# Attention probabilities of the even heads transposed by DMA in a one-core transformer block with routed experts

## The reference, cut to what matters

```
q = LN(x) @ Wq; k, v = split(ctx @ Wkv)          # 16 heads of 64, a null key/value in front
attn = softmax(q * 64**-0.5 @ [nk, k].T)         # 256 x 257 per head
x += tanh(g) * LN(attn @ [nv, v] @ Wout)
x += tanh(g) * ffn_fp8(LN(x))                    # 256 -> 1024 -> 256, relu, fp8 hidden
x += tanh(g) * (rms(LN(x)) @ W_in.T + decayed patch scan of ctx)
x += tanh(g) * top2_experts(LN(x))               # 8 experts, gelu gate
```

## Time and profile before

| | |
|---|---|
| median of 3 runs | 1578.78 us (1574.91 to 1578.94) |
| the profiled execution | 1575.19 us, span 1573.4 us |
| PE busy | 1455.4 us, 92% of the span |
| DVE busy | 1200.8 us, 76% |
| ACT busy | 927.6 us, 59% |
| POOL busy | 635.8 us, 40% |
| mean granted TensorE clock | 0.981 |
| DMA | 93.44 MB, mean 59 GB/s |

### The profile page before, as it was taken

One profiled execution on the slowest core, in us unless ns is written; L12 is line 12 of the kernel. 1 busy time (PEld: TensorE's weight loads), 2 busy tenths in 40 slices (PEclk: granted clock), 3 DMA queues, 4 the chain that ended last, 5 costly groups with the idle time before them and its releaser, 6 DMA issues.

```text
span 1573.4 us, 36260 instructions
## 1 busy us (share of the span) xinstructions
PE 1455.4 (92%) x12542; PEld 1073.2 (68%) x12542; DVE 1200.8 (76%) x3275; ACT 927.6 (59%) x2530; POOL 635.8 (40%) x773
## 2 busy tenths in 40 slices
PE   2999999999999999999999999999967899999997
PEld 2667676767677776767677776767645666666665
DVE  6578888898989898888989898888875545454443
ACT  4476676767676767667676767767654432333332
POOL 6201333424342434424242424334234566555553
PEclk7999999999999999999999999999987999999999
DMA  8202020120202020211202020201232634333231
GB/s 265 86 1 69 10 74 22 61 75 9 81 2 82 2 81 15 69 49 34 82 2 81 2 82 8 75 23 41 73 109 91 188 65 64 57 61 53 50 61 22
DMA packets 78176, 93.44 MB, mean 59 GB/s; under 512 B 21312, under 2 KB 61776, under 8 KB 78000
## 3 DMA queue, kind: packets, MB, share of 16 engines
q1 hardware_dynamic: 51488, 73.21, 14.0%
q0 software_dynamic: 15680, 17.78, 6.9%
q10 hardware_dynamic: 10832, 0.13, 0.4%
HBM read 60.70 MB, written 31.30 MB: 58 GB/s over the span
## 4 chain that ended last, share of the span: by engine, by line
PE 52%; DVE 32%; ACT 9%; issue 4%; DMA 1%; POOL 1%; ACTq 0%; SPq 0%; POOLq 0%; DVEq 0%
PE S L1190 11%; PE W L1137 8%; PE W L1139 8%; PE W L1138 7%; DVE mx L1796 6%; PE O L1212 5%; PE T L1142 5%; ACT prob L956 4%; DVE pTl L1808 3%; PE O L1303 3%; PE S L1275 2%; PE W L1142 2%; DVE st_ln L1767 1%; DVE nm L1799 1%; ACT prob L965 1%
## 5 line engine op out<-in xcount | busy, mean ns | idle before, releaser
L956 ACT ACTIVATE prob<-S,nm 128x256 f32<-128x256 f32 x512 | 235.9, 475 | 88.0 <-DVE nm L1799 87.7
L753 POOL TENSOR_SCALAR ve_ln<-mv_ln 128x2 f32<-128x2 f32 x64 | 14.4, 225 | 534.5 <-DVE mv_ln L1770 534.5
L949 ACT ACTIVATE pTh<-T 128x512 f16<-128x512 f32 x256 | 139.4, 596 | 115.9 <-PE T L1142 107.9
L1808 DVE SCALAR_TENSOR_TENSOR pTl<-T,pTh 128x512 f16<-128x512 f32 x256 | 164.1, 680 | 9.9 <-ACT pTh L949 9.9
L1796 DVE TENSOR_REDUCE mx<-S 128x2 f32<-128x512 f32 x256 | 163.1, 678 | 9.1 <-PE S L1275 9.0
L1190 PE MATMUL S<-GL,xgh 128*128 x568 | 168.9, 379 | 0.1
L716 POOL DMA_INDIRECT out_dram<-ysb,tab x71 | 112.6, 1586 | 114.7 <-issue 67.0
L965 ACT ACTIVATE prob<-prob,rden 128x256 f32<-128x256 f32 x256 | 116.2, 501 | 71.3 <-DVE p0n L1817 71.3
L1142 PE MATMUL T<-ident,prob 128*128 128x128 f32 x1024 | 141.9, 283 | 0.4 <-DVE prob L1823 0.3
L1137 PE MATMUL W<-cTh,Wkh 128*128 128x256 f16 x512 | 140.5, 274 | 0.0
L1138 PE MATMUL W<-cTl,Wkh 128*128 128x256 f16 x512 | 140.5, 274 | 0.0
(11 more groups left out here) (311 smaller groups left out, 4364.3 us busy)
## 6 DMA issues: line engine op xcount, KB each, us to landing
cx<-in_ctx_dram SPq DMA_DIRECT2D x16, 512.0 KB, 5.3
gst<-in_L_ffn_gating_w_dram SPq DMA_DIRECT2D x16, 512.0 KB, 6.2
gating_split<-gsp SPq DMA_DIRECT2D x16, 512.0 KB, 2.7
GL<-gating_split SPq DMA_DIRECT2D x8, 1024.0 KB, 5.2
stg<-in_L_xattn_Wkv_dram SPq DMA_DIRECT2D x8, 512.0 KB, 13.5
xl<-in_x_dram SPq DMA_DIRECT2D x16, 256.0 KB, 4.2
lst<-in_L_ffn_linear_w_dram SPq DMA_DIRECT2D x16, 256.0 KB, 5.2
xres<-in_x_dram SPq DMA_DIRECT2D x16, 256.0 KB, 2.7
```

Source lines behind the costliest of these rows:

```text
L949: A(flat(pTh[:, h, :, :]), T[h][:, :], ACT.Copy).then_inc(s_pTh[h], 1)
L956: ins = A(prob[:, h, t, :], S[h][:, t * NTOK:(t + 1) * NTOK], ACT.Exp, bias=nm[:, h, t:t + 1], scale=SM, accum_out=rs[:, h, t:t + 1])
L1808: V.scalar_tensor_tensor(flat(pTl[:, h, :, :]), T[h][:, :], 1.0, flat(pTh[:, h, :, :]), ALU.mult, ALU.subtract).then_inc(s_pTl[h], 1)
```

## The change

The even head's probabilities no longer go through PE. ACT's `norm` writes them normalized as fp16 high rows (ph) from prob and rden, ahead of the odd head's normalization; DVE's new `even_prob_low` writes the low rows (pl). The sync queue transposes both by two DMAs of 128x512 fp16, SBUF to SBUF, into eTh and eTl, which are double over the pairs. `values` waits for the two DMAs and for the odd head's pTl. The odd head stays as it was: four transposes, one pTh, one pTl. DVE no longer normalizes the even head.

In the order of the engines: `even_prob_low(j)` is placed in each slot, in slots 1 and 5 behind add_residual and decayed, in slots 2 and 4 ahead of attn_low, in slot 7 behind the fourth norm. In slot 2 x1T's high and low parts move ahead of the norm; in slot 3 the norm stands between the two halves of the relus (before: ahead of all four); in slot 7 x4T's copy moves ahead of v's last high part. SP's transfers are spread over the pairs, since each pair now has its two waits there.

Five buffers share homes: sq with hq, x2 with x1, xhTh/xhTl with x1Th/x1Tl, dech with onehot, decl with cum.

```diff
-        pTh, pTl = sb("pTh", [P, 2, 2, NTOK], FP16), sb("pTl", [P, 2, 2, NTOK], FP16)
+        pTh, pTl = sb("pTh", [P, 2, NTOK], FP16), sb("pTl", [P, 2, NTOK], FP16)
+        eTh, eTl = [], []
+        for i in range(2):
+            eTh.append(sb(f"eTh{i}", [P, TT, 2, P], FP16))
+            eTl.append(sb(f"eTl{i}", [P, TT, 2, P], FP16))
+        ph, pl = sb("ph", [P, TT, NTOK], FP16), sb("pl", [P, TT, NTOK], FP16)
...
+            def even_probs_T(g):
+
+                at_least(sp, s_pv, g - 1)
+                sp.wait_ge(s_ph, g + 1)
+                sp.dma_start_transpose(eTh[g % 2][:, :, :, :].rearrange("p t k r -> p (t k) r"),
+                                       ph[:, :, :].rearrange("p t k -> p (t k)")).then_inc(s_eTh[g % 2], 16)
+                sp.wait_ge(s_pl, g + 1)
+                sp.dma_start_transpose(eTl[g % 2][:, :, :, :].rearrange("p t k r -> p (t k) r"),
+                                       pl[:, :, :].rearrange("p t k -> p (t k)")).then_inc(s_eTl[g % 2], 16)
...
+                for j in range(PAIRS):
+                    g = i.n * PAIRS + j
+                    if j == 0 and i.n > 0:
+                        gating_out(i.n - 1, gates_of[i.n - 1])
+                    if j == 1:
+                        if i.n > 0:
+                            linear_out(i.n - 1)
+                        if i.n > 1:
+                            x4_out(post.shift(-1))
+                    if j == 2:
+                        if i.n == 0:
+                            sp.wait_ge(s_setup, 1)
+                        sp.dma_start(lst[:, :, :], pick(lin_v, i.n)).then_inc(s_lw, 16)
+                        if loads:
+                            sp.wait_ge(s_nrm["ln1"], i.n + 1)
+                            sp.dma_start(xl[nxt.par][:, :, :], pick(x_v, nxt.n)).then_inc(s_x[nxt.par], 16)
+                    if j == 3 and loads:
+                        sp.wait_ge(s_u, i.n + 1)
+                        sp.dma_start(cx[nxt.par][:, :, :], pick(ctx_v, nxt.n)).then_inc(s_c[nxt.par], 16)
+                    if j == 4:
+                        sp.dma_start(gst[:, :, :], pick(gat_v, i.n)).then_inc(s_gw, 16)
+                    if j == 5:
+                        if post_:
+                            sp.wait_ge(s_xb, i.n)
+                        sp.dma_start(xres[:, :, :], pick(x_v, i.n)).then_inc(s_xr, 16)
+                    if not pre and j in (3, 5, 6):
...
+                        expert_in((3, 5, 6).index(j))
+                    if j == PAIRS - 1 and post_:
+                        x3_out(post)
+                    even_probs_T(g)
...
                 def norm(j):
-                    act.wait_ge(s_rden, i.n * 8 + j + 1)
+                    g = i.n * PAIRS + j
+                    act.wait_ge(s_rden, g + 1)
+                    at_least(act, s_eTh[(g - 1) % 2], 16 * ((g - 1) // 2 + 1))
+                    for t in range(TT):
+                        ins = A(ph[:, t, :], prob[:, 0, t, :], ACT.Copy, scale=rden[:, 0, t:t + 1])
+                    ins.then_inc(s_ph, 1)
                     for t in range(TT):
                         ins = A(prob[:, 1, t, :], prob[:, 1, t, :], ACT.Copy, scale=rden[:, 1, t:t + 1])
-                    ins.then_inc(s_prob[1], 1)
+                    ins.then_inc(s_prob, 1)
...
+                    g = i.n * PAIRS + j
+                    pe.wait_ge(s_eTh[g % 2], 16 * (g // 2 + 1))
+                    pe.wait_ge(s_eTl[g % 2], 16 * (g // 2 + 1))
+                    pe.wait_ge(s_pTl, g + 1)
...
+                                if h:
+                                    rhs = (pTl if n == 1 else pTh)[:, kt, :].rearrange("p (t r) -> p t r", r=P)
+                                else:
+                                    rhs = (eTl if n == 1 else eTh)[g % 2][:, :, kt, :]
...
+                def even_prob_low(j):
+                    g = i.n * PAIRS + j
+                    at_least(dve, s_eTl[(g - 1) % 2], 16 * ((g - 1) // 2 + 1))
+                    dve.wait_ge(s_ph, g + 1)
+                    for t in range(TT):
+                        ins = V.scalar_tensor_tensor(pl[:, t, :], prob[:, 0, t, :], rden[:, 0, t:t + 1],
+                                                     ph[:, t, :], ALU.mult, ALU.subtract)
+                    ins.then_inc(s_pl, 1)
...
-                    for t in range(TT):
-                        ins = V.tensor_scalar(prob[:, 0, t, :], prob[:, 0, t, :], rden[:, 0, t:t + 1], None, ALU.mult)
-                    ins.then_inc(s_prob[0], 1)
```

More of the change, by code:

```diff
@@ L570, in step @@
                 post, nxt = i.shift(-1), i.shift(2)
+                pre, attn, post_ = PRE in parts, ATTN in parts, POST in parts
+                loads = pre and i.n + 2 < NB
+                if attn:
+                    gates_of[i.n] = work.at["gT"]
                 if i.n == 1:
                     sp.wait_ge(s_blank, 16 * TT * (NB - FIRST_BATCHES))
-                if ATTN in parts and PRE in parts:
-                    wait_apart(sp, s_nrm["ln1"], i.n + 1)
-                    wait_apart(sp, s_u, i.n + 1)
@@ L576, in step @@
[L576 to L611, removed]
+                if not attn:
+                    if i.n == NB:
+                        gating_out(NB - 1, gates_of[NB - 1])
+                        linear_out(NB - 1)
+                        x4_out(post.shift(-1))
+                        sp.wait_ge(s_pv, PAIRS * NB)
+                        sp.wait_ge(s_go, 16 * NB)
+                        sp.wait_ge(s_lo, 16 * NB)
+                        for e in range(early, E):
+                            expert_in(e)
+                        x3_out(post)
+                        x4_out(post)
+                    if loads:
+                        sp.dma_start(xl[nxt.par][:, :, :], pick(x_v, nxt.n)).then_inc(s_x[nxt.par], 16)
+                        sp.dma_start(cx[nxt.par][:, :, :], pick(ctx_v, nxt.n)).then_inc(s_c[nxt.par], 16)
+                    return
@@ L945, in prob_high @@
                 def prob_high(j):
[L946 to L949, removed]
+                    act.wait_ge(s_pT, i.n * 8 + j + 1)
+                    at_least(act, s_pv, i.n * 8 + j)
+                    A(flat(pTh[:, :, :]), T[1][:, :], ACT.Copy).then_inc(s_pTh, 1)
                 def exps(j):
@@ L981, in v_high, with relus @@
                     one("v", m, vh[nxt.par][:, m // 2, (m % 2) * 512:(m % 2 + 1) * 512], 1 / WS)
-                def relus():
-                    for m in range(4):
+                def relus(units=(0, 1, 2, 3)):
+                    for m in units:
                         k, nfull, _ = work.at["w1"][m]
@@ L1069, in step @@
                             k_high(1)
+                        if post_:
+                            one("x1T", 0, flat(x1Th[:, :, :]))
                         if attn:
@@ L1075, in step @@
                             attn_high(0)
-                        if post_:
-                            one("x1T", 0, flat(x1Th[:, :, :]))
                         if pre:
@@ L1080, in step @@
                             q_high(3)
-                    if j == 3 and post_:
-                        relus()
+                    if j == 3:
+                        if post_:
+                            relus((0, 1))
+                        if attn:
+                            norm(j)
+                        if post_:
+                            relus((2, 3))
                     if j == 4:
@@ L2064, in step @@
                             pick_boundaries()
-                    if j == 3 and post_:
-                        boundaries()
+                    if j == 3:
+                        if attn:
+                            even_prob_low(j)
+                        if post_:
+                            boundaries()
                     if j == 4:
```

95 lines of the change are left out of this document (57 added, 38 removed).

## The result

The changed kernel took 1625.65 us, the median of 4 executions (1619.95 to 1631.56), and the kernel before, on the same chip, 1576.85 (1574.05 to 1578.94). The ratio is 1.031, with a 95% interval of 1.027 to 1.035: 49 us slower, where 9.5 us faster was forecast. 1626 lies above the range as well.

What follows compares the result with a forecast made beforehand. PE looked like the bound (68.9 of 71.5 us a step) with DVE close behind. 14 steps at 0.6 us gave 8.4, about 1 more came from step 0, 0 from step 15: 1578.8 - 9.5 = 1569 us, range 1540 to 1612.

Steps and rivals of the forecast that it cites:

- the price of even_prob_low: DVE's two low-row operations a pair were taken at 0.80 us, bounds 0.52 and 1.43 (slowed while POOL writes).
- the walk: Follows one full step from msel through each pair's maxima to the next msel; 9.5 us faster overall, chance 0.42.
- the sum of -0.6 us a step: At the next msel, a full step was to end 0.6 us earlier; 14 such steps give 8.4 us.
- The first and the sixth: Starts of the maxima of pairs 1 and 6, forecast at +0.27 and -0.1 us against before.
- 775.3 against 773.2: End of pair 7's values if transposes take 5 us to land, against before; given as +2.2 us a step.
- the terms of maxima(7): Before pair 7's maxima: division done 758.3, ph, odd norm, vh, aTh 2.8, aTl 0.6; given as +0.3 us.
- The landing L: From end of even_prob_low until values may start: 3.2 us, bounds 1.9 and 6; with 3.2 nothing waits.
- The queueing term: Part of the landing time: 0.3 us for the low rows' transfer queueing on SP, issue taken as some 0.33 us.
- The list of covers: Landing time each slot stands without delay: 3.3 to 5.0 us, slot 7 (3.45) said to go first.
- rival (2): Transposes land late: gain gone from 4.0 us, at 5 us +2.2 a step and 1610 us; chance 0.27.
- Rival (1): PE is the bound after all, ACT and DVE having more slack: -3.7 us a step, 1519 us; chance 0.12.
- No change: Landing between 3.6 and 4.2 us, or ACT's extra work cancelling DVE's saving: 1575 to 1583 us; chance 0.17.

Runs made afterwards that it cites:

- pool_quiet: Changed kernel with GpSimd's xb, x2b, uh, ul, lst, lsp, dech and decl operations cut to 16 columns from step 2 on; 1587.3 us, ratio 1.009.
- before_quiet: Kernel before the change with the same GpSimd operations as in pool_quiet cut to 16 columns from step 2 on; 1565.1 us, ratio 0.994.
- no_transfers: Changed kernel without its 256 transposing DMAs, even values reading the odd head's transposed rows; ph and pl still written; 1606.7 us, ratio 1.020.
- short_both: no_transfers with both ph and pl over 16 of 256 columns; 1559.5 us, ratio 0.991.
- short_low: no_transfers with even_prob_low (pl) over 16 of its 256 columns; 1576.8 us, ratio 1.000.
- short_high: no_transfers with ACT's ph over 16 of 256 columns from step 1 on, pl whole; 1578.0 us, ratio 1.0015.
- rest_alone: Changed kernel without ph and pl, both heads transposed on TensorE as before; shared homes, spread loads and new order kept; 1580.3 us, ratio 1.004.

## Why the prediction was wrong

**The sum was made per engine with durations of undisturbed rows.** The step that failed is the price of even_prob_low and of DVE's operations around it in the walk, and with it the sum of -0.6 us a step. Its 0.80 us is right in six of the eight slots of the step (0.85 to 0.88 by duration, as in the row at 739.08) and wrong in slot 4 (1.24) and slot 5 (1.69, above even the bound of 1.43). The wait for ph ahead of it was seen by the walk in part only: 1.74 us of idle DVE in slot 3 and 1.05 in slot 6 of this step. The walk took every other duration as it stood in before, but xn went from 0.73 to 1.24, dec from 0.85 to 1.07 and xh from 1.43 to 1.56. xn shows how: POOL's xb add starts 7.91 us behind msel in both kernels, but xn started 9.07 behind it and now starts at 8.55, since the even normalization ahead of it is gone. The 0.52 us that the change saved there moved xn into POOL's add, and 0.51 were paid back at once. In the kernel before the two rows are (DVE's timeline, then POOL's)

```profile
710.52 0.73 DVE L1777 TENSOR_SCALAR xn<-xl,mv_ln,rstd_ln 128x256 f32<-128x256 f32 x2
```

```profile
709.36 1.41 POOL L775 TENSOR_TENSOR xb<-xres,bi_b 128x256 f32<-128x256 f32 x2
```

The cause is shown by pool_quiet against before_quiet: 29 of the 49 us.

The trace fits a lock that is held for a whole instruction: over the run a slowed operation ends a fixed time behind the end of a POOL instruction, den 0.02 us, p0n 0.03, xn and xh 0.15, pl 0.28 (30 of 39 slowed ones), dec 0.55. pTl runs beside POOL too and keeps its 0.68. The exception is the second pl of slot 4, nine times over the run: in the walked step it takes 0.83 us and ends 0.60 ahead of POOL's dec (773.34). For it the rule isn't shown. The Trainium skill, "SBUF — State Buffer", SBUF: two separate sides, states such a rule: a DVE operation with two SBUF inputs and a GpSimd operation that reads SBUF take the same port pair in turn, and the loser waits. pl, dec, p0n and den agree with it; xn and xh have one tensor input and are slowed as well. The rule speaks against this change, which replaces a pTl that reads PSUM by a pl that reads SBUF twice, and the prediction should have weighed it.

**Point by point**, the starts of the maxima against before, aligned at msel (before at 701.45 + 27.91 = 729.36), forecast and measured. The third row is pool_quiet against before_quiet, in the same step, where pool_quiet has the full clock and no wait for a landing:

| | maxima(1) | (2) | (3) | (4) | (5) | (6) | (7) | next msel |
|---|---|---|---|---|---|---|---|---|
| forecast, us | +0.27 | 0 | +0.4 | -0.4 | +0.2 | -0.1 | +0.3 | -0.6 |
| measured, us | +0.78 | +0.83 | +1.1 | +0.18 | +0.44 | +1.6 | +2.0 | +1.4 |
| GpSimd quiet, us | +0.27 | +0.07 | +0.33 | -0.60 | +0.20 | -0.14 | -0.36 | -1.02 |

The first and the sixth are the mis-sized ones: +0.5 by xn, and +1.5 in slot 5 by dec, pl and xh. The walk's shape was right, and with GpSimd quiet its numbers are too, to 0.2 us up to maxima(6): what it had wrong is what DVE's operations take beside GpSimd. bnd no longer waits for PE, as forecast; the +0.7 and more of slots 1 to 3 is partly taken back at maxima(4), and PE's saving is lost where the walk lost it, at xh: PE idle 1.43 us there in this step, "near 1" forecast, now joined by 1.14 ahead of logits. Two slips in the prediction's sums change nothing: 775.3 against 773.2 is 2.1, not 2.2, and the terms of maxima(7) give +0.2, not +0.3.

**The landing L.** Forecast 3.2 us; 2.4 to 2.5 in the median, plus the wake-up, for which the forecast took 0.2 us from no row (in the changed kernel PE starts 0.09 us behind the landing that it waited for), so the central value was on the safe side. The queueing term was mis-sized in another place: SP needs 1.20 us to issue one transpose, not the 0.33 of the earlier trace rows, and beside GpSimd's scatters they land in up to 9.5 us, beyond the bound of 6. PE waited for them 28 us in 11 places by the list of waits, and 7.5 us in four more that the profile puts down to "issue", though each ends 0.09 us behind a landing of eTl. Nothing of this was forecast in slots 0 to 6, and it was in slot 3 that it came in 11 of the steps 2 to 14, not in slot 7. The list of covers said so: slots 1 and 3 had the least, 3.3 us, and slot 7 had 3.45. Of 1309 ns a block (the Trainium skill, "VectorE: DVE Perf Modes", The three transpose paths) this trace shows less than half: four blocks land 2.4 us after the issue, near the 2.1 us of a plain transfer of twice the bytes out of SBUF, as the Trainium skill, "Advanced Engine Details and Errata", X-Bar Transpose (TRN2), has it.

**What rival (2) got right.** It ended on the slower side by a mechanism that exists: with waits in PE, ACT and DVE it is worth up to 19 us. It is the smaller part. Its 1610 was reached without it: no_transfers is at 1606.7.

**The clock** was no term of the walk. Behind idle gaps of 1.43 us ahead of xhT and 1.14 ahead of logits came at least 2.4 us at the 1.2 GHz level. It was left at nothing without a reason, though the walk itself forecast a longer idle gap of PE: in no_transfers a step with such a stretch takes 1.3 us more than one without.

**Rival (1)** fell: PE as the bound would give 1519, and even short_both gives 1559.5. **No change** would have been met only by work that is left out (short_low, short_high).

The steps between the runs are 6 us the rest of the change, 26 ph and pl net of TensorE's saving, 9 the transfers with ACT's and DVE's waits for them, 10 PE's waiting for them. That they add up to the difference says nothing, since each run starts where the last one ends. The 29 us of meeting GpSimd, and what the clock costs, cut across these parts and aren't added to them. What stays open: the order on ACT that costs rest_alone its 6 us was read from the trace, and no run undid it alone.

No version of the changed kernel came out faster than the one before. The one that did, short_both, leaves the split out.

## What to carry to other kernels

Before moving work from a TensorE-and-PSUM path onto SBUF operands, lay the timeline of POOL under that of DVE: here an operation on SBUF that met a POOL instruction mostly lasted until a little behind that one's end, operations of four columns too. Where two engines are nearly level, work taken from the busier one is worth only what the other can follow, and time saved on one can move its next operation into a meeting with POOL. Here two cheap additions (0.95 us on ACT, 0.87 on DVE a pair) in one chain cost more than twice what half the transposes were worth (47 us by short_both against no_transfers, and 21 by short_both against rest_alone). An experiment that takes work away from an engine needs the same edit in the kernel before as its control, since it moves what stands behind.

## What the runs showed of the hardware

- A DMA transpose of 128x512 fp16 within SBUF occupies SP's queue for 1.20 us (20 of the 256 for 1.3 to 3.6; a plain one for 0.57 in the median) and lands 2.4 us after its issue; 256 of them raise the run's packets from 78176 to 217440, 160576 of these under 512 B:

```profile
DMA packets 217440, 126.99 MB, mean 78 GB/s; under 512 B 160576, under 2 KB 201040, under 8 KB 217264
```

- Beside four indirect scatters on GpSimd they landed after 9.5 and 8.4 us; with the scatters left out, after 4.7 and 4.1 at most.
- DVE's p0n of 12 columns took 1.01 us in place of 0.18 beside a POOL subtraction of 1.16 us.
- DVE operations that read only SBUF and met a POOL instruction ended a fixed time behind its end (den 0.02 us, xn and xh 0.15, pl 0.28, dec 0.55), with slot 4's second pl as the exception; pTl, which reads PSUM, kept its 0.68 us beside POOL.
- Leaving out four scatters a step on GpSimd made the kernel before 17 us slower, 12 of them by POOL work that moved beside DVE's division.
- A step with a stretch at the 1.2 GHz level took 1.3 us more than one without (74.1 and 72.8 us in no_transfers).
